# Eight layers on one core: row scores among the projections, Silu and Tanh in a test-time MLP, look-ups turned a group sooner

## The reference, cut to what matters

```python
def _L1_attn_ref(x, W_Q, W_KV, W1, b1, W2, b2):        # test-time MLP
    def _mlp(params, h):
        return jax.nn.silu(h @ W1 + b1) @ W2 + b2
    def loss_fn(params, k_t, v_t):
        return jnp.mean((_mlp(params, k_t) - v_t) ** 2)
    def step(params, kvt):                              # one step per position, 1024 of them
        g = jax.grad(loss_fn)(params, k_t, v_t)
        return tuple(p - LR * gp for p, gp in zip(params, g)), None
    ...
    return _mlp(params, x @ W_Q)

def _L2_attn_ref(...):    # 8 heads of 16; softmax(q k / 4) v, with biases
    scores = jnp.einsum('bhsd,bhtd->bhst', q, k) / jnp.sqrt(dk)
    p = jax.nn.softmax(scores, axis=-1)

def _L3_attn_ref(...):    # 16 heads of 8; running maxima over blocks of 64 keys
    m_new = jnp.maximum(m, M_ij)
    corr = jnp.exp(m - m_new)

def _L3_ffn_ref(...):     # shared expert, and two of eight routed experts per row
```

## Time and profile before

| | us |
|---|---|
| median of 3 runs | 2502.32 (2501.33 to 2507.28) |
| the profiled execution | 2503.04 |
| its span, first to last instruction | 2501.2 |
| PE, DVE, ACT, POOL busy | 2040.6, 1846.2, 1281.2, 540.2 |
| test-time MLP, first and last Sigmoid (tile tt_sg) | 510.6 to 865.6 |
| first attention: first projection, first landed maxima | 1064.4, 1146.0 |
| second attention: the same | 1610.5, 1686.7 |
| look-ups: first turning to last gather | 2447.5 to 2488.1 |

### The profile page before, as it was taken

The page is one execution under the profiler, slowest core; times in us unless marked ns, Lnnn a source line. Parts: engine busy times, 40 slices in busy tenths (PEclk is TensorE's granted clock), DMA queues, the critical chain, the costliest instruction groups (busy, mean ns, idle before and its releaser), DMA issues.

```text
span 2501.2 us, 63690 instructions
## 1 busy us (share of the span) xinstructions
PE 2040.6 (82%) x19949; PEld 1145.6 (46%) x20012; DVE 1846.2 (74%) x3716; ACT 1281.2 (51%) x2708; POOL 540.2 (22%) x1121
## 2 busy tenths in 40 slices
PE   4449884788888778648999997649999999999876
PEld 2336562467777643223444444423333333333454
DVE  5865767755655557847888886659999999999575
ACT  4311114533333230144777776438888888888621
POOL 4322233134444410200111111101111111111300
PEclk9755557999999978877999998769999999999977
DMA  2342210000000000031111110031111111111001
GB/s 58 83 124 71 70 46 18 8 1 0 0 0 0 0 10 0 12 101 39 33 32 32 32 35 8 16 107 38 38 39 39 38 39 38 39 39 39 10 20 34
DMA packets 140886, 86.67 MB, mean 35 GB/s; under 512 B 67339, under 2 KB 120212, under 8 KB 140757
## 3 DMA queue, kind: packets, MB, share of 16 engines
q1 hardware_dynamic: 140756, 84.95, 13.3%
HBM read 57.01 MB, written 27.26 MB: 34 GB/s over the span
## 4 chain that ended last, share of the span: by engine, by line
PE 50%; DVE 16%; issue 5%; ACT 5%; DMA 2%; SPq 1%; POOL 0%; DVEq 0%; another core or an unknown queue 0%; POOLq 0%; ACTq 0%; PEldq 0%
PE psum L2282 13%; PE psum L2260 12%; PE psum L2271 8%; DVE ba_blockmax L2525 5%; DVE X L1424 2%; PE psum L2291 2%; ACT tt_sg L1786 1%; DVE tt_aT L1841 1%; PE psum L1745 1%; PE psum L1754 1%; PE psum L1735 1%; SPq L2187 1%; PE psum L1352 1%; DVE row_stats L148 1%; PE psum L1764 1%
## 5 line engine op out<-in xcount | busy, mean ns | idle before, releaser
L2525 DVE TENSOR_REDUCE ba_blockmax<-psum 128x16 f32<-128x1024 f32 x512 | 602.2, 1218 | 35.2 <-PE psum L2260 32.5
L2364 ACT ACTIVATE ba_pt<-psum 128x512 f32<-128x512 f32 x1024 | 550.5, 598 | 71.2 <-PE psum L2271 53.0
L2260 PE MATMUL psum<-ba_ks,ba_qs 64*128 64x512 bf16 x1024 | 342.0, 414 | 39.4 <-DMA ba_ks<-ba_kstk 19.4
L2527 DVE TENSOR_REDUCE sa_negmax<-psum 128x1 f32<-128x1024 f32 x256 | 304.3, 1220 | 85.7 <-PE psum L2260 77.9
L2364 ACT ACTIVATE sa_pt<-psum 128x512 f32<-128x512 f32 x512 | 269.7, 599 | 116.4 <-remote 59.0
L2282 PE MATMUL psum<-ba_pt,ba_vh 128*32 128x256 f32 x4096 | 314.6, 390 | 0.1
L2271 PE MATMUL psum<-ba_qs,ba_ks 64*128 64x512 bf16 x1024 | 313.6, 381 | 0.8 <-ACT ba_pt L2364 0.8
L2260 PE MATMUL psum<-sa_ks,sa_qs 96*128 96x512 bf16 x512 | 207.0, 409 | 30.2 <-DMA sa_ks<-sa_kstk 22.9
L2260 PEld LDWEIGHTS psum<-ba_ks,ba_qs 64*128 64x128 bf16 x1024 | 113.0, 149 | 231.4 <-issue 228.7
L2271 PE MATMUL psum<-sa_qs,sa_ks 128*128 128x512 bf16 x449 | 170.3, 382 | 1.8 <-ACT sa_pt L2364 1.6
L2282 PEld LDWEIGHTS psum<-ba_pt,ba_vh 128*32 128x32 f32 x4096 | 92.3, 108 | 154.6 <-issue 146.7
(11 more groups left out here) (447 smaller groups left out, 3852.1 us busy)
## 6 DMA issues: line engine op xcount, KB each, us to landing
ba_qs<-ba_qstk SPq DMA_DIRECT2D x128, 48.0 KB
ba_ks<-ba_kstk SPq DMA_DIRECT2D x128, 48.0 KB
dn_pst<-dn_arena SPq DMA_DIRECT2D x32, 128.0 KB, 2.5
dn_tst<-dn_arena SPq DMA_DIRECT2D x8, 512.0 KB, 5.9
dn_arena<-dn_tst SPq DMA_DIRECT2D x8, 512.0 KB, 4.3
dn_arena<-dn_pst SPq DMA_DIRECT2D x8, 512.0 KB, 6.2
ba_qs<-ba_qstk SPq DMA_DIRECT2D x128, 32.0 KB
ba_ks<-ba_kstk SPq DMA_DIRECT2D x128, 32.0 KB
```

Of the source, the lines that this page charges most:

```text
L2260: last = nc.tensor.matmul(bank(2 * slot + h), qs[b][0:KP, :].rearrange("p (a r) -> p r a", r=NTB)[:, r, :], ks[b][0:KP, h * HALF:(h + 1) * ...
L2364: nc.scalar.activation(pt[x_][:, :, h * P:(h + 1) * P].rearrange("p j (a m) -> p j a m", m=2), bank(4 + slot).rearrange("p (a j m) -> p j ...
L2525: ins = nc.vector.tensor_reduce(blockmax[g][:, r, :], src.rearrange("p (n s) -> p n s", s=BLOCK), AXX, ALU.max, negate=True)
L2527: ins = nc.vector.tensor_reduce(negmax[g][:, r:r + 1], src, AXX, ALU.max, negate=True)
```

## The change

In the MLP ScalarE computes `aT` itself with Silu, and then Tanh of half the sum in place of the Sigmoid. `sg` now holds tanh(z/2) = 2 sigmoid(z) - 1, so sp becomes twice the slope, and the factor of L1857 is halved. The Tanh needs half of b1, which VectorE makes once a chunk.

In both attentions the row scores of the first ten rows go between the projection steps 3 to 7, two a step, all into banks 0 and 1; row R waits for the maximum of row R - 1. VectorE takes the first of a step's two maxima behind the copy of v and the second behind the rest. SP loads head 0 after the first two stores have landed, and the others between later stores. The loops over the batches are unrolled. The maxima of head 0 are brought in ahead of the wait for all stores.

In the look-ups TensorE turns group g + 1 ahead of looking up group g.

```diff
         def scalar(self, a):
-            nc.scalar.activation(sgq[0][0:1, 0:1], k.mhalf[0:1, 0:1], ACT.Sigmoid).then_inc(self.table, 1)
+            nc.scalar.activation(sgq[0][0:1, 0:1], k.mhalf[0:1, 0:1], ACT.Silu).then_inc(self.table, 1)
...
                     a.wait_ge(self.sp, n + 1)
-                    nc.scalar.activation(sg[:, :], bank(HB)[:, 0:P], ACT.Sigmoid, bias=b1).then_inc(self.sig, 1)
+                    nc.scalar.activation(aT[:, :], bank(HB)[:, 0:P], ACT.Silu, bias=b1).then_inc(self.a, 1)
+                    if s == 0:
+                        a.wait_ge(self.half_b1, c + 1)
+                    nc.scalar.activation(sg[:, :], bank(HB)[:, 0:P], ACT.Tanh, bias=b1h[:, :], scale=0.5).then_inc(self.sig, 1)
...
                     v.wait_ge(self.sig, n + 1)
-                    nc.vector.scalar_tensor_tensor(aT[:, :], bank(HB)[:, 0:P], b1, sg[:, :], ALU.add, ALU.mult).then_inc(self.a, 1)
                     v.wait_ge(self.a, n + 1)
...
-                    nc.vector.tensor_tensor(sp[:, :], sg[:, :], tsp[:, :], ALU.subtract).then_inc(self.sp, 1)
+                    nc.vector.scalar_tensor_tensor(sp[:, :], sg[:, :], 1.0, tsp[:, :], ALU.add, ALU.subtract).then_inc(self.sp, 1)
...
-                    nc.vector.scalar_tensor_tensor(r[:, 3 * P:4 * P], bank(DB)[:, 0:P], -ETA, r[:, 0:P], ALU.mult, ALU.mult).then_inc(self.dh, 1)
+                    nc.vector.scalar_tensor_tensor(r[:, 3 * P:4 * P], bank(DB)[:, 0:P], -ETA / 2, r[:, 0:P], ALU.mult, ALU.mult).then_inc(self.dh, 1)
...
+                half_bias(c + 1)
+
+            def half_bias(c):
+                v.wait_ge(self.weights1, c + 1)
+                nc.vector.tensor_scalar(b1h[:, :], b1, 0.5, None, ALU.mult).then_inc(self.half_b1, 1)
```

```diff
+    EARLY = {3: (0, 1), 4: (2, 3), 5: (4, 5), 6: (6, 7), 7: (8, 9)}
+    N_EARLY = 10
...
+    def row_bank(n, r):
+        return 0 if n.ramp and n.c * NTB + r < N_EARLY else 2 * (r % 2)
...
+        def first_load(c, at, landed):
+            s.wait_ge(cleared, c + 1)
+            load(Head(0, c), at, landed)
+
+        store(0, 0)
+        store(0, 1)
+        for g in range(2):
+            s.wait_ge(stored[g], 6 * 16 + 1)
+            k.plain(s)
+        first_load(0, 0, loaded)
+        store(1, 0)
+        first_load(1, 0, loaded)
+        store(1, 1)
         if blocked:
+            first_load(0, K0, key_loaded)
+        store(2, 0)
+        if blocked:
+            first_load(1, K0, key_loaded)
+        store(2, 1)
+        if blocked:
+            first_load(2, 0, loaded)
+        store(3, 0)
+        store(3, 1)
         maxima(Head(0, 0))
+        s.wait_ge(cleared, 4)
+        for g in range(2):
+            s.wait_ge(stored[g], B * 6 * 16 + 1)
...
+        def ramp(R):
+            n = Head(0, R // NTB, True)
             if R % NTB == 0:
                 t.wait_ge(loaded[n.c], 96)
+            if 0 < R <= N_EARLY:
+                t.wait_ge(rows_free[(R - 1) % 2], (R - 1) // 2 + 2)
             for h in range(2):
                 rows_scores(n, R % NTB, h)
...
+        for step in range(2 * B):
+            project(step // 2, step % 2)
+            for R in EARLY.get(step, ()):
+                if R == 0:
+                    for g in range(2):
+                        t.wait_ge(xt[g], B + 1)
+                ramp(R)
+        for g in range(2):
+            t.wait_ge(rest_in[g], B + 1)
+            t.wait_ge(v_in[g], B + 1)
+        for R in range(N_EARLY, LEAD):
+            ramp(R)
```

```diff
         t.wait_ge(table_in, 1)
+        spread(0)
         for g in range(NG):
-            spread(g)
+            if g < NG - 1:
+                spread(g + 1)
             look_up(g)
             if g >= 2:
                 gather(g - 2)
```

More of the change, by code:

```diff
@@ L2008, with __init__ @@
 class Head:
-    def __init__(self, i, c):
-        self.i, self.c = i, c
+    def __init__(self, i, c, ramp=False):
+        self.i, self.c, self.ramp = i, c, ramp
     def of(self, per, add=0, by=1):
@@ L2388, in gpsimd @@
         p.wait_ge(cleared, 4)
-        for g in range(2):
-            p.wait_ge(v_in[g], B + 1)
         def split_max(n):
@@ L2461, in gpsimd @@
         split_max(Head(0, 0))
+        for g in range(2):
+            p.wait_ge(v_in[g], B + 1)
         stage_v(Head(0, 0))
@@ L2582, in body, with ramp, take @@
                         finish(n.at(-1))
-        for R in range(LEAD):
-            row_max(Head(0, R // NTB), R % NTB)
+        def ramp(R):
+            row_max(Head(0, R // NTB, True), R % NTB)
             if R == NTB and blocked:
                 negative(Head(0, 0))
+        def take(i, g, between):
+            v.wait_ge(projected[g], i + 1)
+            src = bank(4 + 3 * g).rearrange("p (m h e) -> p h m e", m=GROUP, h=H)
+            dst = vall[:, i * H:(i + 1) * H, g * GROUP:(g + 1) * GROUP, 0:HD]
+            if blocked:
+                nc.vector.tensor_copy(dst, src).then_inc(v_in[g], 1)
+            else:
+                more = bv_all[:, :].rearrange("p (h e) -> p h e", h=H).unsqueeze(2).to_broadcast([P, H, GROUP, HD])
+                nc.vector.tensor_tensor(dst, src, more, ALU.add).then_inc(v_in[g], 1)
+            for R in between[0:1]:
+                ramp(R)
+            v.wait_ge(upper_in[g], i * 2 + 2)
+            for z, n in enumerate("qk"):
+                if blocked:
+                    c_.do(nc.vector.tensor_tensor(rest[n][g][:, :], bank(2 + 3 * g + z), parts[n][g][:, 0, :], ALU.subtract))
+                else:
+                    c_.do(nc.vector.scalar_tensor_tensor(rest[n][g][:, :], bank(2 + 3 * g + z), bias[:, z:z + 1], parts[n][g][:, 0, :],
+                                                         ALU.add, ALU.subtract))
+            c_.sync()
+            v.sem_inc(rest_in[g], 1)
+            for R in between[1:2]:
+                ramp(R)
+            v.wait_ge(middle_in[g], i * 2 + 2)
+            for n in "qk":
+                c_.do(nc.vector.tensor_tensor(parts[n][g][:, 2, :], rest[n][g][:, :], parts[n][g][:, 1, :], ALU.subtract))
+            c_.restart()
+            v.sem_inc(split[g], 1)
+        for step in range(2 * B):
+            take(step // 2, step % 2, EARLY.get(step, ()))
+        for R in range(N_EARLY, LEAD):
+            ramp(R)
         heads(v, body)
```

90 lines of the change are left out of this document (25 added, 65 removed).

## The result

The changed kernel takes 2461.17 us (median of 4 runs, 2460.14 to 2462.42) where the kernel before, on the same chip, took 2503.76 (4 runs, 2501.33 to 2507.28): a ratio of 0.983, interval 0.981 to 0.985, 42.6 us less. The forecast was 2472; the range of 2460 to 2489 holds the result, 1.2 us above its lower end. The profiled execution took 2460.21 us, its span is 2458.4 (before 2501.2).

A forecast was written before the change was run, and what follows sets the result against it. No engine was full in the MLP's hopping chain, and the attentions' ramps ran two phases in series; steady loops stay. Gains 10.5 + 10.6 + 7.7 + 1.8 = 30.6 us off 2503.04 gave a forecast of 2472 us, range 2460 to 2489.

The forecast's parts named there:

- MLP, 10.5 us forecast: Test-time MLP loop: Silu and Tanh on ScalarE shorten the chain by 10.5 us, bounds 5.5 and 16.
- The third sweep's term: MLP chunk, third sweep: TensorE gets aT earlier and turns sp sooner; gain 0.32 us.
- The second sweep: MLP chunk, second sweep: tsp waits for GpSimd's addition and ends at the same time; gain 0, upper bound 0.10 us.
- The first sweep's term: MLP chunk, first sweep: Tanh waits for half of b1, ready at about 0.35 us; gain 0.02, bounds -0.07 and 0.10.
- The table load, 0 forecast: Function tables around the MLP loop: a 1.28 us load is covered by ScalarE's 2.93 us idle; cost 0, uncovered 1.3.
- First ramp, 10.6 forecast: First attention's ramp: rows among the projections lose 7.5 us there but shorten the tail; gain 10.6 us, bounds 3.3 and 13.6.
- The bound of 13.6: First attention's ramp: upper bound of the gain, with rows and projections at full clock and shorter issues of fixed addresses.
- Second ramp, 7.7 forecast: Second attention's ramp: same layout with its own durations and delayed loads; gain 7.7 us, bounds 0.5 and 11.
- The first rival's half clock: Both ramps: TensorE stays at half clock, so they give 3.8 us, not 18.3; time 2487, chance 0.14.
- Look-ups, 1.8 forecast: Look-ups at the end: 0.7 us won in the first groups, 1.1 at the last, steady period kept; bounds 0 and 2.5.
- the rival "more": MLP and ramps: a fixed charge in the second sweep and full clock in both ramps; time 2461, chance 0.05.
- the rival on the MLP: MLP loop: its gain does not come, as sp is as late as before; time 2483, chance 0.10.

The follow-up runs named there:

- e5: GpSimd's third addition in the MLP loop made to wait for the second sweep's sp, against the changed kernel: 2447.38 us.
- e7: Silu straight on ScalarE in the MLP layer's queries' phase, with a one-element Silu ahead of the waits, against the changed kernel: 2459.69 us.
- e4: Only the batch loops in both attentions' ramps unrolled, no row taken ahead, against the kernel before: 2497.77 us.
- e6: Eight early rows from projection step 4 on, in place of ten from step 3, against the changed kernel: 2451.22 us.
- e2: The change's part in the ramps of both attentions alone, against the kernel before: 2475.79 us.
- e3: The change's new order of the look-ups alone, against the kernel before: 2500.47 us.
- e1: The change's MLP part alone (Silu, Tanh, half bias), against the kernel before: 2487.48 us.
- e10: Later GpSimd addition, early rows from step 4, seven more products of zeros before the first look-up, against the changed kernel: 2437.17 us.
- e12: Later GpSimd addition, early rows from step 4, products of zeros before the look-ups, throwaway products before row 0, against the changed kernel: 2435.85 us.

## Why the prediction was right, and where it was off

**MLP, 10.5 us forecast, 12.7 measured.** The third sweep's term was right in size (0.32 forecast, 0.29 measured at the last product) and in its steps: sp's turning at 1.34 us (1.35 said), the last product at 2.18 (2.15 said), Tanh's end at 0.63 (0.65). The second sweep gave nothing, as said, for the reason said: e5 shows that tsp waits for GpSimd. The Trainium skill (SBUF — State Buffer, "Who interferes with whom") says that a VectorE instruction with two SBUF inputs contends with a GpSimd instruction that reads SBUF. The rows agree: tsp takes 0.50 or 0.64 us beside the addition, by where it starts, and 0.29 away from it. The first sweep's term was mis-sized, 0.02 forecast and 0.11 measured (chunk's sum 11.20 to 10.80): the half of b1 was ready 0.26 us behind the Silu's start, not 0.35, so the Tanh started 0.30 us behind the Silu, where it is 0.27 in the other sweeps. The gain of 0.11 is also past the bound of 0.10 given for it. The lower bound for the whole loop, 5.5, can't be worked out from the terms, which give 7.7.

**The table load, 0 forecast.** The step named one load and covered it by 2.93 us of idle time. There are two, of 1.28 us, since the copy behind the branch brings one of its own, and the first did not start until TensorE's product was there. The first Sigmoid came 0.7 us later, counted from the loop's last sweep; on the way to the next layer nothing of it is seen (198.8 us before, 198.4 after), as e7 shows from the other side.

**First ramp, 10.6 forecast, 16.2 measured.** The mechanism is as laid out: the load ahead of the third store, VectorE's stand for row 0, the last step late (54.4 to 57.4 us) and the long tail gone (27.2 to 8.0). Four terms were too dear. Step 3's rest began at 27.9 us, not 29.0. Step 4's projection ended at 33.6, not 35.6, for its clock rose in the middle. Steps 5 to 7 took 5.9, 6.3 and 5.9 us, not 6.4 each: I had kept the stores as their bound, and with fixed addresses VectorE's own 5.9 is what is left. And the last store and the maxima took 8.0, with the 1 us that I had added for delay 9.6. The bound of 13.6, made of full clock and shorter issues, was too low by 2.6: e4 prices the unrolling alone at 3.1 us. These accounts overlap, and I can't part them further. The gain came out half as large again as the term.

**Second ramp, 7.7 forecast, 9.5 measured.** The right size, but by two errors that nearly cancel, which is luck. The first rival's half clock came true here in a part of each of the steps 4 to 7; against it I had said that no gap of some 3.6 us is left behind step 4, and none is: the longest wait before a row there is 1.42 us.

```profile
1612.56 0.65 PE L2273 MATMUL psum<-ba_ks,ba_qs 64*128 64x512 bf16 x2
1614.63 0.62 PE L2273 MATMUL psum<-ba_ks,ba_qs 64*128 64x512 bf16 x2 [1.42 <-DVE ba_blockmax L2539]
...
1616.49 1.92 PE L2348 MATMUL psum<-XT,ba_wk 128*128 128x512 f32 x2
```

The two rows ran at full clock, and the projection of step 5 behind them at half (1.92 us; 1.02 at full). So a gap of that length isn't needed for the clock to fall. It costs 1.3 us a step (7.1 us) against the 5.8 that e6 has between its steps 5 and 6. On the other side, hops and issues were shorter, as in the first ramp (e4: 2.2 us here).

**Look-ups, 1.8 forecast, 4.8 in the two traces, 2.4 at like clock.** From the first turning to the end the trace of before has 53.7 us, e2 and e4 51.7 and 51.8, the changed kernel 48.9, e3 and e7 49.2. (What lies ahead of it in the table's last stretch was 1.4 us longer in the changed kernel, so the stretch shows 3.4.) From the first gather to the end it was 40.0 us before, in e1, e2 and e4, and is 38.8 in the changed kernel: 1.2 us, where 1.1 was said for the last weighing, and the steady period stayed, as said. To the first gather 1.2 us were won where I had 0.7. The rest of that stretch's difference is the clock: the profiled execution of before rose late, so I took its 3.72 us as the look-up's price and as nothing that could change.

The time lies at the number of the rival "more", 2461, and neither of its reasons held: no fixed charge, no full clock in both ramps. By the prediction's own bounds these two give 3.1 and 6.3 us, so 2463; 2461 takes the MLP's upper bound of 16 whole. And the 2483 of the rival on the MLP is its 10.5 us alone: with half of the ramps' doubt (14.5 us) it would be 2490, outside the range. The sum was 30.6 and the two spans differ by 42.8, because nearly all terms erred to the same side: of the 12.2 us between, 2.2 are in the MLP, 5.6 and 1.8 in the ramps, 1.6 in the last stretch and 1.0 in all else.

## What to carry to other kernels

When an instruction is moved ahead on a chain, look at what it then overlaps on another engine: an addition of GpSimd's whose result nobody on the chain waited for cost this loop 10.5 us, until it was made to wait for the second sweep's sp. When work is drawn forward into a pipeline's ramp, start it where its input is surely there; one step too early, VectorE stood for it, in order, with the stores behind it (7.6 us in the second attention). And before a difference of a few us is laid to an edit, look at the same stretch in kernels where its lines are unchanged: TensorE's clock alone moved some here by 2 to 3 us.

## What the runs showed that I had not expected

**The clock's rise differs between executions of the same code.** The queries' phase of the MLP layer has the same lines in the changed kernel and in e6. The rows are the windows 871 to 874 and 874 to 877 us of each, and 877 to 880 of the changed kernel, which stands first; the loop's last activation is at 852.1 and 852.0 us; the number behind the counts is the granted clock.

```profile
871.00:874.00 3.00, 3.00 (x5) 0.83 (x3) 1.06 (x2) 1.37 (x2) 0.00 (x0) 0.50 0.00 0
874.00:877.00 3.00, 3.00 (x11) 2.14 (x10) 0.46 (x2) 0.00 (x0) 0.00 (x0) 0.50 0.00 0
877.00:880.00 3.00, 3.00 (x7) 0.74 (x7) 1.27 (x2) 0.69 (x1) 0.00 (x0) 0.75 0.00 0
```

```profile
871.00:874.00 3.00, 3.00 (x8) 1.03 (x7) 1.38 (x2) 1.38 (x2) 0.00 (x0) 0.81 0.00 0
874.00:877.00 3.00, 3.00 (x14) 1.48 (x14) 1.44 (x3) 0.69 (x1) 0.00 (x0) 1.00 0.00 0
```

TensorE is busy throughout both, and its idle time before, since the loop's end, differs by 0.12 us at most, yet the clock rose from 1.2 to 2.4 GHz in the first window of e6 and in the third of the changed kernel: by the shares 0.81 and 0.75 at 872.1 and 878.5 us, 6.4 us apart. From the loop's end to the next attention the fourteen traces have two values: 198 to 200 us (ten of them, before and after among these) and 195 to 196 (e5, e6, e10, e12). Together with the start of the look-ups (2.1 us) and the end of the kernel (1.95 or 3.58 us for the last products) that is some 3 to 7 us between executions that no edit is needed to explain. It is why a term below that size can be read from its own stretch only, and why a median's difference, such as e1's 17.1, may stand off its trace's 12.5. What decides the moment is open.

**Table sets.** Silu, Tanh and the copies from PSUM needed no load between them in 96 sweeps; Silu and Tanh took what the Sigmoid did (0.37 and 0.36 us, the Sigmoid 0.37), and started 0.26 to 0.29 us apart.
